# Linear attention: the minimum of the keys on VectorE straight from PSUM, and their exponential on ScalarE, both one group ahead of the features

## The reference, cut to what matters

```python
def _feature_map(x):
    return jnp.where(x > 0, x + 1.0, jnp.exp(x))
...
kvp = kv @ Wkv.T
k, v = jnp.split(kvp, 2, axis=-1)
q = _feature_map(...)                      # 16 heads of 16
k = _feature_map(...)
kv_summary = jnp.einsum('bhsd,bhse->bhde', k, v)
k_sum = k.sum(axis=-2)
z = 1.0 / (jnp.einsum('bhld,bhd->bhl', q, k_sum)[..., None] + EPS)
attn = jnp.einsum('bhld,bhde->bhle', q, kv_summary) * z
```

## Time and profile before

| | us |
|---|---|
| median of 3 runs | 3332.2 (3330.4 to 3334.85) |
| the profiled execution's own time | 3334.43 |
| its span | 3332.5 |
| PE busy in the span | 3129.3 (94%) |
| DVE, ACT, POOL busy | 2082.6, 1801.0, 1851.6 |
| linear attention, first key matmul to last product | 63.9 to about 751 |

### The profile page before, as it was taken

One profiled execution on the slowest core, in us unless ns is written; L12 is line 12 of the kernel. 1 busy time (PEld: TensorE's weight loads), 2 busy tenths in 40 slices (PEclk: granted clock), 3 DMA queues, 4 the chain that ended last, 5 costly groups with the idle time before them and its releaser, 6 DMA issues. The chain is left out here.

```text
span 3332.5 us, 65238 instructions
## 1 busy us (share of the span) xinstructions
PE 3129.3 (94%) x23304; PEld 2828.0 (85%) x23304; DVE 2082.6 (62%) x3434; ACT 1801.0 (54%) x3277; POOL 1851.6 (56%) x1890
## 2 busy tenths in 40 slices
PE   5999999996999999579999999999999999995999
PEld 4999999985999999558888888888888888884998
DVE  4666666664222222537777777787778777775554
ACT  2666666651323323146666666666666666662443
POOL 3888888872433434145565656555655655541332
PEclk8999999996999999789999999999999999997999
DMA  4454444421100100011110111011111111104000
GB/s 129 148 148 148 148 148 148 148 74 38 39 20 19 38 19 0 0 61 37 54 54 30 51 54 51 30 54 54 45 35 54 54 37 44 54 13 152 6 6 11
DMA packets 88460, 203.85 MB, mean 61 GB/s; under 512 B 25408, under 2 KB 64688, under 8 KB 83376
## 3 DMA queue, kind: packets, MB, share of 16 engines
q1 hardware_dynamic: 86288, 202.93, 19.4%
q10 hardware_dynamic: 2112, 0.12, 0.1%
HBM read 184.94 MB, written 14.42 MB: 60 GB/s over the span
## 5 line engine op out<-in xcount | busy, mean ns | idle before, releaser
L1448 DVE TENSOR_TENSOR a_probT<-a_p,a_probT 125x448 fp32r<-125x448 f32 x768 | 459.4, 618 | 155.0 <-ACT a_probT L1381 151.9
L1381 ACT CAST a_probT<-a_p 125x448 fp32r<-125x448 f32 x768 | 396.1, 538 | 255.1 <-PE a_p L1565 250.6
L1442 DVE TENSOR_REDUCE a_mxs<-a_s 112x1 f32<-112x1500 f32 x256 | 439.8, 1718 | 96.1 <-PE a_s L1553 92.7
L1580 PE MATMUL a_o<-a_probT,a_val 125*64 125x224 f32 x3072 | 473.1, 277 | 1.7 <-DVE a_probT L1448 0.9
L1565 PE MATMUL a_p<-ident,a_prob 112*125 112x112 f32 x3072 | 438.6, 274 | 2.5 <-DVE a_probT L1448 2.3
L1565 PEld LDWEIGHTS a_p<-ident,a_prob 112*125 112x125 f32 x3072 | 387.7, 188 | 43.7 <-issue 26.7
L1374 ACT ACTIVATE a_prob<-a_s,a_mxs 112x1500 f32<-112x1500 f32 x256 | 389.6, 1522 | 15.7 <-DVE a_mxs L1442 14.6
L438 POOL TENSOR_TENSOR l_rows_lo<-l_raw,l_rows_hi 125x512 fp32r<-125x512 f32 x192 | 344.2, 1793 | 55.7 <-ACT l_rows_hi L475 55.7
L1580 PEld LDWEIGHTS a_o<-a_probT,a_val 125*64 125x64 f32 x3072 | 337.8, 136 | 38.0 <-issue 24.5
L736 POOL TENSOR_TENSOR e_hT_lo<-e_h,e_hT_hi 128x448 fp32r<-128x448 f32 x144 | 168.0, 1167 | 353.1 <-ACT e_hT_hi L783 353.1
L1298 POOL TENSOR_TENSOR a_two<-a_picked 64x224 f32<-64x224 f32 x128 | 84.5, 660 | 432.3 <-DVE a_picked L1460 432.3
(11 more groups left out here) (279 smaller groups left out, 9355.0 us busy)
## 6 DMA issues: line engine op xcount, KB each, us to landing
l_rawT<-in_ctxT SPq DMA_DIRECT2D x32, 1500.0 KB, 6.3
a_rawT<-in_ctxT SPq DMA_DIRECT2D x32, 1500.0 KB, 6.2
l_raw<-in_ctx SPq DMA_DIRECT2D x32, 1344.0 KB
e_gu_in<-in_L_ffn_w_gate_up SPq DMA_DIRECT2D x8, 1024.0 KB, 4.9
W_hi<-w_out_hi SPq DMA_DIRECT2D x32, 192.0 KB, 2.4
W_lo<-w_out_lo SPq DMA_DIRECT2D x32, 192.0 KB, 2.4
l_raw<-in_ctx SPq DMA_DIRECT2D x32, 156.0 KB
e_down_in<-in_L_ffn_w_down SPq DMA_DIRECT2D x8, 512.0 KB, 5.8
```

The costliest lines, as they stand in the source:

```text
L1381: act.copy(p_target(j, f, 0), p_source(i)).then_inc(p_hi[i], 1)
L1442: dve.tensor_reduce(mxs[:, j:j + 1], s_bank[0:TT, :, 0:GW], AX.XY, ALU.max, negate=True).then_inc(max_done, 1)
L1448: dve.tensor_tensor(p_target(j, f, 1), p_source(i), p_target(j, f, 0).bitcast(F32), ALU.subtract).then_inc(p_read[i], 1)
L1580: mm = pe.matmul(o_bank[0:2 * PW, at:at + 2 * TT], flat(val[:, ch, j, :, :]), flat(probT[j % 2][:, ch, :, :]), start=(ch == 0), stop=(ch = ...
```

## The change

The second part of a feature is now exp(min(key, 0)) rather than min(exp(key), 1). DVE's minimum reads the key bank and writes l_expk (new function `minimum`); ACT's exponential reads l_expk and writes it in place (new function `exponential`). Both are done at step g for group g + 1, with one of each ahead of the first batch. So the minimum of group g + 1, with its wait for the keys of group g + 1, stands in front of the features of group g on DVE. DVE's `kv_copy` moves from behind the features of step 0 to in front of them. PE's, POOL's and SP's programs stay as they are.

```diff
 # ScalarE, batch(), step g
-                    act.wait_ge(k_full, NP * b + g + 1)
-                    if g >= 2 or not first:
-                        act.wait_ge(phi_done, NP * b + g - 1)
-                    act.activation(expk[:, g % 2, :], k_bank[g % 2][0:CH, :], ACT.Exp).then_inc(exp_done, 1)
+                    if not (last and g == NP - 1):
+                        exponential(b, g + 1, first)
...
+            def exponential(b, g, first):
+
+                act.wait_ge(min_done, NP * b + g + 1)
+                act.activation(expk[:, g % 2, :], expk[:, g % 2, :], ACT.Exp).then_inc(exp_done, 1)
...
 # VectorE
+            def minimum(b, g, first):
+                dve.wait_ge(k_full, NP * b + g + 1)
+                if g >= 2 or not first:
+                    dve.wait_ge(phi_done, NP * b + g - 1)
+                dve.tensor_scalar(expk[:, g % 2, :], k_bank[g % 2][0:CH, :], 0.0, None, ALU.min).then_inc(min_done, 1)
+
             def batch(b, u, first=False, known=False, last=False):
                 for g in range(NP):
-                    dve.wait_ge(exp_done, NP * b + g + 1)
-                    dve.tensor_scalar(expk[:, g % 2, :], expk[:, g % 2, :], 1.0, None, ALU.min).then_inc(min_done, 1)
+                    if not (last and g == NP - 1):
+                        minimum(b, g + 1, first)
                     if g + 2 < NP:
                         t_low(b, u, g + 2)
                     elif not last:
                         t_low(b + 1, 1 - u, g + 2 - NP)
 
-                    dve.wait_ge(min_done, NP * b + g + 1)
+                    if g == 0 and not first and not known:
+                        kv_copy(b - 2)
+                    dve.wait_ge(exp_done, NP * b + g + 1)
                     if g >= 2 or not first:
                         dve.wait_ge(phi_lo, NP * b + g - 1)
                     dve.scalar_tensor_tensor(out=phif[:, g % 2, :], in0=k_bank[g % 2][0:CH, :], scalar=0.0,
                                              in1=expk[:, g % 2, :], op0=ALU.max, op1=ALU.add).then_inc(phi_done, 1)
-                    if g == 0 and not first and not known:
-                        kv_copy(b - 2)
```

More of the change, by code:

```diff
@@ L491, in _ @@
             t_copy(0, 0, 1)
+            exponential(0, 0, True)
             batch(0, 0, 0, first=True)
@@ L558, in _ @@
             t_low(0, 0, 1)
+            minimum(0, 0, True)
             batch(0, 0, first=True)
```

## The result

| | before | after |
|---|---|---|
| median, us | 3332.8 (3330.4 to 3334.9) | 3440.2 (3437.6 to 3441.4) |
| ratio, 95% interval | | 1.0317 (1.0305 to 1.0329) |
| span of the profiled execution | 3332.5 | 3435.9 |

The change makes the kernel 107 us slower; forecast were 98. The page of the changed kernel; the third row is PE's granted clock in tenths.

What follows compares the result with a forecast made beforehand. The ring of ACT and DVE was taken as the bound. Batches of 24.12 us, 3.14 more than 20.98, gave 94.2 us over 30 batches, 98 in all with the first two: median 3431 us, range 3385 to 3475.

Steps and rivals of the forecast that it cites:

- The ring of ACT and DVE: Kernel before: cast, exponential, minimum, subtraction and features wait in a cycle, 3.51 us a group; PE needs 19.7 of 20.98 a batch.
- PE waits for the bank in four groups of six: Plain groups: next keys wait for features, 2.21 us from the l_g block's start, 0.76 idle; group 3.71 instead of 3.50.
- The price of the minimum: DVE's minimum reading 512 columns of the key bank: taken as 0.67 us, the ends being 0.43 and 0.69.
- The straight line: Estimate of the minimum's time from 0.258 us on 112 columns and 0.68 on 512: 1.05 ns a column, 0.67 us.
- `numden` at 1.94: Step 1: `numden` starts 1.94 us after the l_g block's start, waiting for l_KV; key block to key block 4.35 us.
- `kv` at 2.62, then 0.81: Step 5: `kv` starts 2.62 us after the l_g block's start, waiting for l_GT, and takes 0.81; group 4.93 us.
- POOL, SP and the clock at nothing: Whole stage: POOL's passes fit in 3.71 us, SP reloads as before, PE's clock stays at 1.00; no added time.
- The rival of the clock: PE's pauses lower its clock; one slow stretch in each batch adds 66 us, 3497; chance 0.06.
- The late l_GT: Step 5: ACT's copy for `kv` stands behind group 5's exponential, 1.17 us new wait in each batch.
- The subtraction's hold-up by POOL: Rival: DVE's subtraction waits for POOL's pass; once in a batch by 1.06 us is 33 us, 3464; chance 0.09.
- The last step of the sum: From 3432.5 us for the profiled execution, which lies 2.2 above the median of the runs, to a median of 3431.

Runs made afterwards that it cites:

- swap_only: Kernel before with minimum moved to read the key bank and exponential in place, both still at step g for group g: 3285.7 us.
- experiment 8: Kernel before with DVE's subtraction in front of its in-place minimum, 3565.4 us; then also POOL's row pass cut to 128 of 256 columns, 3460.1 us.
- half_min: Changed kernel with minimum and exponential over the first 256 of 512 columns only, the rest left out: 3386.8 us.
- both_first: Changed kernel with the subtraction in front of the minimum on DVE and the l_GT copy in front of group 5's exponential on ACT: 3427.5 us.
- before_tlow: Kernel before with DVE's subtraction in front of its in-place minimum, nothing exchanged or ahead: 3565.4 us, ratio 1.069.
- before_tlow_half: before_tlow with POOL's row pass doing only the first 128 of each chunk's 256 columns: 3460.1 us.
- edits 3 and 2: Changed kernel with, in 3, ACT's l_GT copy in front of group 5's exponential, 3402.6 us; in 2, minimum and exponential on 256 columns, 3386.8 us.
- edit 5: Also written tlow_first: changed kernel with DVE's subtraction (for group g + 2) in front of the minimum of g + 1: 3418.2 us.

## Why the prediction was right

By its own steps:

- *The ring of ACT and DVE bounds, PE is 1.3 us of a batch below it.* Right in its length: swap_only, which cuts the ring and adds nothing, gains 48 us. Its batch is 19.6 us in the steady state, 1.35 shorter, close to the 19.7 I had added up for PE; the rest of the 48 comes mostly from the first batches. I had one part wrong: the minimum's 0.62 us was its own 0.43 and a hold-up by POOL's feature pass, so the ring of the kernel before went through POOL (experiment 8).
- *PE waits for the bank in four groups of six, 2.21 us from the block of l_g.* Measured 2.22. The price of the minimum, the one unknown, was 0.69 us (forecast 0.67, between 0.43 and 0.69). The straight line that was given for it says no more than its upper point, the features' 0.68 at 512 columns; half_min's 0.42 us at 256 columns lies 0.01 above it.
- *`numden` at 1.94.* Measured 313.21 - 311.14 = 2.07: the start behind l_KV took 0.26 us rather than 0.14 (0.26 in the batch at 801 us too, 0.14 in that at 337). This is 0.13 of a batch.
- *`kv` at 2.62, then 0.81.* Measured 2.60 and 0.92 (305.91 - 304.99): behind a wait the product itself costs 0.11 more than behind other matmuls. With 0.02 more in each plain group these make up the 0.28 us between 24.12 and 24.40, and so the 9 us between forecast and result.
- *POOL, SP and the clock at nothing.* Right: POOL's passes are at 1.29 us without a hold-up, the clock is 1.00 in every window of 100 us of the stage though PE pauses in each group, by 0.2 to 1.0 us. The rival of the clock did not come. A lower clock was seen only in the runs with the longest pauses: 0.97 in the window from 200 to 300 us of both_first (pauses up to 1.8 us), 0.96 in that of before_tlow (up to 2.2 us) and 0.98 in that of before_tlow_half (up to 1.7 us).
- *The rivals.* The late l_GT and the wait for the bank are separate terms, shown by edits 3 and 2 (edit 5, meant for the same, ran into a ring of its own). The subtraction's hold-up by POOL, 0.09 in the forecast, was at most 0.06 us in the changed kernel (0.73 at its longest, 0.67 alone); in both_first, before_tlow and tlow_first it came, with 1.63, 1.36 and 1.37 us.
- *The last step of the sum.* 3432.5 less 2.2 is 3430, not 3431.

What was clearly wrong lay in the experiments: twice I moved an instruction out of one chain without following what it stood behind next, and beside which pass of POOL it would start.

## What to carry to other kernels

An instruction that waits blocks all that stands behind it on its engine. Before work is put ahead, ask whom the work behind it serves: with two banks, whatever frees bank g must not stand behind a wait for the producer of g + 1, or the double buffer is a single one. Put the early work behind the release, not in front of it. And look for the plain edit first: the exchange of the two engines' parts alone, with nothing ahead, took 3285.7 us, the fastest of all versions here, 1.5% below the kernel before.

## What the runs showed of the hardware

- The fp32 minimum over 512 columns on VectorE takes 0.69 us from PSUM and 0.43 us in SBUF undisturbed. In SBUF beside a GpSimd pass it took 0.61 us in the kernel before and 1.50 in before_tlow: each time it ended 0.27 to 0.30 us behind the pass, so it follows that pass's length one to one. The faster form can be the slower one where GpSimd is busy.
- The fp32 subtraction of two SBUF tensors (128 x 500) took 0.67 us alone and up to 1.65 (both_first) beside a GpSimd pass, to 0.52 to 0.55 us behind the pass's end.
- A small product behind a wait on PE took 0.92 us to the next keys, behind other matmuls 0.81.
- PE's clock held its upper level (1.00, 2.4 GHz) in the changed kernel, from 110 to 800 us, over a pause of 0.2 to 1.0 us in every group.
